# Gated heads: the output experts by routing instead of by a product over all eight experts

## The reference, cut to what matters

```python
# L1 gated heads: 8 heads of 64, 8 experts for each head
q = (x @ w_q).reshape(b, n, 8, 64); k = (x @ w_k).reshape(b, n, 8, 64)
gates = sigmoid((x @ w_gate).reshape(b, n, 8, 8))
gm = one_hot(argmax(gates)) * gates                 # one expert per token and head
values = einsum('bhne,ehdk,bnd->bhnk', gm, value_experts, x)
attn = softmax(causal(q * 64**-0.5 @ k.T))
out = einsum('bhij,bhjk->bhik', attn, values)
out = einsum('bhne,ehkd,bhnk->bhnd', gm, output_experts, out)
x = x + out.sum(heads)
# L0 expert layer, the part touched: gate_logits = tokens @ gate_w.T  (8 experts, top 2)
```

## Time and profile before

| | |
|---|---|
| profiled execution, its own time | 3965.39 us |
| its span | 3963.7 us |
| gated heads begin (POOL's first instruction in them) | 2772.85 us |
| busy over the span | PE 91%, weight loads 76%, DVE 74%, ACT 55%, POOL 8% |
| granted PE clock over the span | 0.964 |
| DMA | 109.74 MB, mean 28 GB/s |
| SP's copies of 128 rows in L0's expert stage, issue to landing | median 2.1 us (L806), 1.9 us (L810) |

### The profile page before, as it was taken

How to read it: one execution, slowest core, us unless ns; L and a number is a source line. 1 busy time by engine, 2 the same in 40 slices (tenths; PEclk the granted TensorE clock), 3 DMA queues, 4 the chain that set the end, 5 groups by cost and what they waited for, 6 DMA issues and landing times. The chain is left out here.

```text
span 3963.7 us, 93437 instructions
## 1 busy us (share of the span) xinstructions
PE 3604.9 (91%) x28994; PEld 2998.0 (76%) x28994; DVE 2943.2 (74%) x9189; ACT 2170.0 (55%) x6661; POOL 299.0 (8%) x382
## 2 busy tenths in 40 slices
PE   6999999899999998269967889998899999999998
PEld 5888888688888887259845666665688888888887
DVE  5666666677777776546558878887888888888886
ACT  5767777677777774135444557776433333333333
POOL 0000000000000000431188000000000000000000
PEclk9999999899999998579989999999999999999999
DMA  2000000100000003332211000000200000000000
GB/s 98 0 0 0 0 0 0 38 33 11 11 11 11 11 11 102 110 109 78 67 55 42 0 20 21 21 21 15 95 9 16 8 11 13 8 11 13 11 11 9
DMA packets 56112, 109.74 MB, mean 28 GB/s; under 512 B 8368, under 2 KB 27184, under 8 KB 55728
## 3 DMA queue, kind: packets, MB, share of 16 engines
q1 hardware_dynamic: 46656, 80.72, 6.5%
q0 software_dynamic: 8464, 26.22, 2.0%
q10 hardware_dynamic: 864, 1.19, 0.1%
HBM read 72.46 MB, written 35.65 MB: 27 GB/s over the span
## 5 line engine op out<-in xcount | busy, mean ns | idle before, releaser
L639 ACT ACTIVATE c_pr<-c_sm,c_nmx 128x256 f32<-128x256 f32 x512 | 254.5, 499 | 153.6 <-DVE c_nmx L485 153.6
L127 PE MATMUL f_ps_out<-f_out_rounded,f_zgT 128*128 128x256 f32 x1024 | 309.7, 302 | 0.0
L128 PE MATMUL f_ps_out<-f_out_rest,f_zgT 128*128 128x256 f32 x1024 | 288.1, 281 | 0.0
L129 PE MATMUL f_ps_out<-f_out_rounded,f_zgT 128*128 128x256 f32 x1024 | 285.9, 279 | 0.0
L639 ACT ACTIVATE a_pr<-a_sm,a_nmx 128x128 f32<-128x128 f32 (+1 forms) x512 | 227.3, 445 | 106.3 <-DVE a_nmx L485 106.2
L485 DVE CUSTOM_DVE_ANT_0 a_sm<-a_ps_s,causal 128x128 f32<-128x128 f32 (+1 forms) x512 | 152.6, 355 | 164.2 <-PE a_ps_s L371 164.2
L2156 DVE TENSOR_REDUCE f_v<-f_gv 128x64 f32<-128x512 f32 x256 | 269.0, 1051 | 0.4
L1747 ACT ACTIVATE c_pr<-c_ps_s,c_nmx 128x256 f32<-128x256 f32 x512 | 214.2, 500 | 88.2 <-DVE c_nmx L1579 88.2
L485 DVE CUSTOM_DVE_ANT_0 c_sm<-c_ps_s,c_mask 128x256 f32<-128x256 f32 x512 | 186.8, 421 | 92.0 <-PE c_ps_s L371 90.4
L2306 ACT CAST f_zgT<-f_ps_g 128x512 fp32r<-128x512 f32 x256 | 151.3, 591 | 182.4 <-PE f_ps_g L2036 182.4
L2147 DVE TENSOR_TENSOR f_gv<-f_ps_v,f_gm_step 128x512 f32<-128x512 f32 x256 | 175.5, 685 | 97.5 <-PE f_ps_v L129 86.0
(11 more groups left out here) (377 smaller groups left out, 11405.2 us busy)
## 6 DMA issues: line engine op xcount, KB each, us to landing
f_slot_rows<-f_run POOLq DMA_DIRECT2D x1, 9216.0 KB, 34.5
f_rows<-f_slot_rows SPq DMA_DIRECT2D x72, 128.0 KB, 2.1
f_slot_out<-f_y SPq DMA_DIRECT2D x72, 128.0 KB, 1.9
c_ctx_stage<-in_ctxT SPq DMA_DIRECT2D x32, 256.0 KB, 2.7
small<-in_f_w SPq DMA_DIRECT2D x16, 512.0 KB
x_sb<-in_x SPq DMA_DIRECT2D x8, 512.0 KB, 8.0
small<-in_c_w SPq DMA_DIRECT2D x8, 512.0 KB, 3.7
c_mask_stage<-in_mask SPq DMA_DIRECT2D x16, 256.0 KB, 2.9
```

The source lines that it names most:

```text
L127: nc.tensor.matmul(out, sh, mh, start=start, stop=False, **kw)
L128: nc.tensor.matmul(out, sh, ml, start=False, stop=False, **kw)
L129: return nc.tensor.matmul(out, sl, mh, start=False, stop=stop, **kw)
L639: last = nc.scalar.activation(pr[:, r, i, 0:n], sm[:, j, i, 0:n], ACT.Exp, bias=nmx[:, j, i:i + 1], scale=-1.0, accum_out=sums[:, r, i:i + 1])
```

## The change

The gated heads are written anew around the output experts; the L0 gate is turned over.

- Order of the steps: batches go in four groups of four, and a **phase** is one pair of heads for the four batches of a group. There are 16 phases of 4 steps. The tokens of a group stay in SBUF (`xs`), so x is read and turned for a whole group ahead of its phases; from the second group on it is read twice, once for the gates and once for the values.
- Values: the same products, but the columns are laid out with the expert innermost, so that `sum_v` reads neighbouring elements, and the gate's value is taken out of them: `gate_v` multiplies by the one-hot choice, and the value of the gate goes into the copy of the probabilities (`take_prT`) and into `scale`. The probabilities are no longer divided on DVE: the inverse of the sum is in `scale`, with which `take_z` multiplies.
- Output: each row (token and head) is sent by an indexed transfer to a slot in DRAM, sorted by expert, with its 64 values twice (512 bytes). A phase has 15 **blocks** of 128 slots for each of its two heads, and a block has one expert. For a block SP loads the rows, PE turns them (two transposes), ACT and DVE split them, PE multiplies with the weights of the block's expert (four products of 256 columns, the expert's number read from a register), ACT copies the result out, and SP stores it. Indexed transfers that add into SBUF bring the rows back to `x_sum`.
- For this the gates' choices are counted: products with a triangle and with ones (`count`), running sums, slots and owners (`index`), all small.
- q and k are made by `product3` of rounded parts in place of four products of full precision.
- The loop over steps is written out: 77 slots, of which the last 13 have no step of their own.
- L0 gate: the gate weights are the stationary side and 256 tokens the moving side, six products a batch; ACT copies the 8 x 256 result and PE turns it back by two transposes, two batches later.

The diff, cut to its core:

```diff
@@ routed_experts, PE: the L0 gate
-                for i in range(ST):
-                    n = ST * b + i
-                    for dc in range(DC):
-                        last = product3(nc, ps_l[:, n * E:(n + 1) * E], [a[:, b % 2, dc, i * P:(i + 1) * P] for a in tT],
-                                        [a[:, dc, :] for a in gate_w], dc == 0, dc == DC - 1)
-                last.then_inc(gated, 1)
+                if b >= 2:
+                    pe.wait_ge(lT_ready, b - 1)
+                for dc in range(DC):
+                    last = product3(nc, ps_h[b % 2][0:E, 0:S], [a[:, dc, :] for a in gate_w],
+                                    [a[:, b % 2, dc, :] for a in tT], dc == 0, dc == DC - 1)
+                last.then_inc(gated, 1)
+            def turn_gates(b):
+                pe.wait_ge(lT_ready, b + 1)
+                for i in range(ST):
+                    n = ST * b + i
+                    last = nc.tensor.transpose(ps_l[:, n * E:(n + 1) * E], lT[:, b % 2, i * P:(i + 1) * P], c.ident[0:E, 0:E])
@@ gated_heads, POOL
+            def scatter(n):
+                pool.wait_ge(indexed, 2 * (n // GB) + 2)
+                pool.wait_ge(z_ready, n + 1)
+                for i in range(ST):
+                    for j in range(2):
+                        t = ST * part(n) + i
+                        pool.indirect_dma_start(rows_z, bass.IndirectOffsetOnAxis(ap=slot_at[:, n // GB % (2 * ROUND), t, j:j + 1], axis=0),
+                                                zr[:, i, j].rearrange("p u k -> p (u k)"), None).then_inc(scattered, 16)
+            def gather(q, k):
+                ...
+                for t in range(half * TG // 2, half * TG // 2 + TG // 2):
+                    done = HEADS * g + 2 * p + j
+                    if done:
+                        pool.wait_ge(summed[t], 16 * done)
+                    pool.indirect_dma_start(x_sum[:, t, :], None, rows_y[q % ROUND],
+                                            bass.IndirectOffsetOnAxis(ap=result_at[:, q % (2 * ROUND), t, j:j + 1], axis=0),
+                                            compute_op=ALU.add).then_inc(summed[t], 16)
+            for n in range(LAST):
+                if 0 <= n - 4 < N:
+                    scatter(n - 4)
+                if 0 <= n - GATHER_AT < N:
+                    gather((n - GATHER_AT) // GB, (n - GATHER_AT) % GB)
@@ gated_heads, PE
-                for p in range(E // 2):
-                    last = product3(nc, ps_out[:, i * D:(i + 1) * D], [t[:, k % 2, p, :] for t in zgT],
-                                    [t[:, 2 * s + j, p, :] for t in w_out], s == 0 and k == 0 and p == 0, ...)
+            def turn_rows(n, step, late_half):
+                pe.wait_ge(rows_in[n % RR], 16 * (n // RR + 1))
+                if n:
+                    pe.wait_ge(sT_ready, n)
+                ...
+                for j in range(2):
+                    last = nc.tensor.transpose(ps_s[0][:, j * P:(j + 1) * P], rows[:, n % RR, j, :], c.ident[:])
+            def experts(n, owner_of):
+                pe.wait_ge(sT_ready, n + 1)
+                if n >= 2:
+                    pe.wait_ge(y_ready, n - 1)
+                for j in range(2):
+                    e = owner_of(j * BLOCKS + m)
+                    for h in range(2):
+                        last = nc.tensor.matmul(ps_y[n % 2][:, j * D:(j + 1) * D], sT[:, h, j, :],
+                                                w_out[:, bass.ds(e + (2 * p + j) * E, 1), :].rearrange("p a d -> p (a d)"),
+                                                start=(h == 0), stop=(h == 1))
+            turn_x(job_at[-GB], -1)
+            for b in range(GB):
+                gates(b)
+                if b + 1 < GB:
+                    turn_x(job_at[b + 1 - GB], -1)
+            for n in range(LAST):    # q, m = (n - 9) // 4, four blocks a slot; at m == 0: pe.load of the owners
+                if now: project(n)
+                blocks(0)
+                if now: project_v(n, 0)
+                ... values(n - 3), turn(n - 2, 0); blocks(1); project_v(n, 1); turn(n - 2, 1); scores(n - 1)
+                ... project_v(n, 2); blocks(2); project_v(n, 3); blocks(3); back(n - 3); gates; count
@@ gated_heads, DVE
-        gv = sb("gv", [P, 2, E, 64])
+        gv = sb("gv", [P, 64, E])
+            def take_z(n):
+                dve.wait_ge(backed, n + 1)
+                dve.wait_ge(scaled, n + 1)
+                if n:
+                    dve.wait_ge(scattered, 64 * n)
+                ...
```

More of the change, by code:

```diff
@@ L1239, in small_heads @@
         if not softmax:
-            gathered = [sem(f"gathered{i}") for i in range(ST)]
+            gathered = [c.kept.enter_context(nc.semaphore(f"{tag}_gathered{i}")) for i in range(ST)]
             weighted = sem("weighted")
@@ new lines, in gated_heads @@
+        chosen_pos = sb("chosen_pos", [P, 2, TG, HEADS])
+        full = sb("full", [P, HEADS, E])
+        ends = [sb(f"ends{n}", [P, HEADS, 4 + E]) for n in range(3)]
+        end = sb("end", [P, 2, HEADS, E])
+        first_row = sb("first_row", [P, 2, HEADS, E])
+        half_of = sb("half_of", [P, HEADS // 2, 2])
+        at = work[:, ST * HEADS * E:].rearrange("p (t j e) -> p t j e", t=TG, j=2)
+        at_sum = sb("at_sum", [P, TG, 2])
+        slot_at = sb("slot_at", [P, 2 * ROUND, TG, 2], U32)
@@ new lines, in _, with blocks @@
+            normalise(0)
+            dve.wait_ge(made, 14)
+            for b in range(GB):
+                rest_x(b)
+                if b + 1 < GB:
+                    normalise(b + 1)
+                choose(b)
+                if b == 0:
+                    rest_qk(0)
+                if b < AHEAD:
+                    pieces.rest(nc, dve, b, b + 1)
+            dve.wait_ge(made_round, 2)
+            for n in range(LAST):
+                def blocks(k):
+                    if (it := place(n, k)) is not None and it[1] < BLOCKS:
+                        rest_rows(it[0] * BLOCKS + it[1])
+                now = n < N
+                if n - 1 in count_at:
+                    take_count(count_at[n - 1])
+                if n in index_at:
+                    index(index_at[n])
+                if 0 <= n - 4 < N:
+                    take_z(n - 4)
+                if 0 <= n - 2 < N:
+                    scale_of(n - 2)
+                blocks(0)
+                if now:
+                    gate_v(n, 0)
+                    sum_v(n, 0)
+                if n in qk_at:
+                    rest_qk(qk_at[n])
+                blocks(1)
+                if now:
+                    gate_v(n, 1)
+                if 0 <= n - 1 < N:
+                    row_max(n - 1, 0)
+                if now:
+                    sum_v(n, 1)
+                if 0 <= n - 1 < N:
+                    row_max(n - 1, 1)
+                if now:
+                    gate_v(n, 2)
+                if n in job_at and job_at[n][2]:
+                    rest_x(job_at[n][3])
+                if now:
+                    sum_v(n, 2)
+                blocks(2)
+                if now:
+                    gate_v(n, 3)
+                blocks(3)
+                if now:
+                    sum_v(n, 3)
+                if n in choose_at:
+                    choose(choose_at[n])
+                if n + 1 in job_at:
+                    normalise(job_at[n + 1][0])
+                pieces.rest(nc, dve, 2 * n + AHEAD, 2 * n + AHEAD + 2)
@@ L2543 @@
     y = nc.dram_tensor("f0_slot_out", (72, P, D), F32, kind="Internal").ap()
-    program(nc, dram, mid, slots, y, out)
+    y1 = [nc.dram_tensor(f"f1_slot_out{n}", (15, P, 2 * D), F32, kind="Internal").ap() for n in range(4)]
+    program(nc, dram, mid, slots, y, y1, out)
     r = run_bass_kernel_spmd(nc, [arrays], core_ids=[0])
```

929 lines of the change are left out of this document (570 added, 359 removed).

## The result

The changed kernel took 4086.07 us in the median of four runs (4078.14 to 4092.36), the kernel before 3972.92 beside it: a ratio of 1.0281 (1.0255 to 1.0308), slower by 2.8%. The forecast was 3740, with 8% for slower. The profiled execution has a span of 4089.3 us. In two later sets of runs, in which the kernel before took 3954 and 3953 us in place of 3973, the same changed kernel was 1.0067 (1.0051 to 1.0084) and 1.0070 (1.0054 to 1.0087) of it. So 2.1 points of the 2.8 depend on where it ran. The forecast of 5.9% less was wrong in both places: where the ratio was 1.007, the span was 3991 us against 3737.

A forecast was written before the change was run, and what follows sets the result against it. PE was taken as the bound, with DVE close under it. 2797.5 + 9 x 11 + 55 x 13.5 + 10 + 106 - 18 = 3737 us span, stated as 3740; own range 3700 to 3785, 8 in 10 within 3665 to 3850.

The forecast's parts named there:

- I add 0.4 a slot: 13.5: Gated heads from the tenth slot: PE and DVE waiting on each other adds 0.4 us to PE's 13.1.
- Work of PE and DVE a slot: Gated heads: PE 13.1 us a slot with blocks, 9.9 without; DVE 10.8, or 11.6 with dependent sums.
- Blocks: Gated heads from the tenth slot: 15 blocks in four slots, 2.6 us of PE a slot plus 0.4 coupling.
- the load of registers: Start of each phase: loading the owners' registers, mostly covered by the projection, 0.6 us times 16, 10 in all.
- POOL's price: Indexed transfers, eight a slot: 1.27 us each, adding ones priced like plain ones, 10.2 a slot, hidden under 13.5.
- rival 2: POOL becomes the bound: an adding gather costs 0.97 more, 2.24 us; a slot 14.0, total 3800; 14%.
- Rivals 2 and 4: The second of these: POOL's adding gathers alone make it slower, 3965 us at 2.9 each, 4145 at 3.6; 8%.
- Rival 3: Gated heads: PE and DVE wait on each other, no engine full, 15.2 us a slot from the tenth, 3830; 21%.
- First nine slots: Start of the gated heads, no blocks or second gates: PE 9.9 us, taken as 11 a slot for DVE's weight splitting.
- First projection: Start of the gated heads: four batches turned ahead instead of one, 15.6 us later, at 2797.5 before L0's saving.
- L0's gate: L0 expert stage: 18 us saved, from 14 at PE's 1.2 GHz to 24 if the clock is at 2.4.
- The end: After the last step: 106 us; last phase's 15 blocks at 2.35 each, done at 80, then four gathers, 20.

The follow-up runs named there:

- after_again: The changed kernel run once more, unaltered, beside a kernel before at 3954 us: 3982.22 us, 1.0067 of it.
- spread2: Changed kernel with rows requested earlier, DVE's output ahead of count and index, small DVE operations spread out, x stores/loads and choice reordered: 3826.69 us, 0.9687 of before.
- early_rows: Changed kernel with SyncE asking for a phase's first three blocks of rows during the phase ahead's last steps: 3904.53 us, 0.9870 of the kernel before.

## Why the prediction was wrong, step by step

**The step that failed** is "I add 0.4 a slot: 13.5", an average coupling for every slot. Just ahead of it stands that slots with `index`, `choose` or `take_count` "put 3 to 5 us more on DVE", and that only two quarters' value products can be buffered; it was not drawn from this that PE waits for nearly all of it. The slot with gates and index has 6.3 us of DVE operations ahead of `take_z`, and PE stood 4.6. In `after_again` the slots with gates cost 117 us over 13.5 and the phases' first ones 56; in `spread2` the same slots are 37 and 1 over. The mended orders took 142 of the 952.5 us of the 55 slots away with the same work.

- Work of PE and DVE a slot: near. Without blocks plain slots are 10.5, the shortest 9.9, against 9.9; with them 13.7 against 12.9 (the 13.5 less the 0.6 of gates and turning). DVE was busy 10.6 us a slot from the tenth on (580 us in `after_again`) against 10.8, and `sum_v` was at 0.68 in the first profile, where the earlier trace rows had led to 0.69:

```profile
L2471 DVE TENSOR_REDUCE f_v<-f_gv 128x64 f32<-128x512 f32 x193 | 131.7, 682 | 17.4 <-PE f_ps_z L2262 12.3 <-issue 2.6 <-DVE f_gv L2462 0.2
```

- Blocks: 3.2 us a slot against 3.0, in plain slots. At the start of a phase the prediction looked for the cost in the load of registers (10 us in all); it was SyncE's order: 4 to 5 us of wait a phase, and 5.9 us of these slots (19.1 to 13.2 in `early_rows`). That a request stands behind a store in a queue could be read from the code; the prediction followed no queue of SyncE.
- POOL's price: the adding transfer is 1.56 + 0.30, not 1.27, between the forecast and rival 2's 2.24. The Trainium skill (Collectives: The Full Stack, the part on why ReduceScatter is half of AllGather) speaks of two source reads for an add. The prediction had read that as twice the length on POOL; it grew to 1.6 times (1.56 against 0.96). Rivals 2 and 4 did not happen: a slot of POOL is 4 x 1.27 + 4 x 1.86 = 12.5 of 13.7, close, but never what ended a wait of the steps.
- Rival 3 had the right sign, both engines under 88%, and the wrong picture and size: an even 15.2 (3830), where it was 13.7 with slots of 19 to 24 between.
- First nine slots: 125 against 99. Slots 4, 6 and 8 (counted from 0), with gates, are 21.2, 21.0 and 19.5 us beside neighbours of 10.5 and 11.0. PE waits 21.6 us for `f_zr` in the nine, behind the same row of DVE operations, uncounted there; in `spread2` it is 7.9, and the nine take 115.5. The rest of the 26 was not taken apart.
- First projection: the forecast went by a kernel before of the first place, so it is to be held against 2782.2 there: 3 us late, by two errors that nearly cancel, which is luck. L0's gate gave 24 us and not 18, and so the turning of four batches in place of one took about 24 us more and not 15.6 (2782.2 - 2781.9 + 24). For L0 the granted clock rose to full in the third batch (24 was the bound for that case). The first row is the stretch at the gates (clock 0.82, where the earlier trace rows had 0.50), the others are starts of the turning of x: 3.5 us for two batches where the earlier trace rows had 3.33 for one.

```profile
1552.00:1572.00 20.00, 17.87 (x116) 11.98 (x116) 15.30 (x43) 11.70 (x31) 0.29 (x1) 0.82 1.01 342
```

```profile
1562.25 0.66 PE L879 MATMUL f_ps_x<-ident,f_t 128*128 128x128 f32 x4
1563.76 0.66 PE L879 MATMUL f_ps_x<-ident,f_t 128*128 128x128 f32 x4
1565.76 0.66 PE L879 MATMUL f_ps_x<-ident,f_t 128*128 128x128 f32 x4
```

- The end: 149 against 106. The 15 last blocks run alone at 2.9 us each where 2.35 were counted (the terms named for it add up to 2.4). PE is at 1.2 GHz there (clock 0.50): from the start of a block's turning to ACT it is 0.7, and the products take 1.0 to the next turning, where 0.6 was counted for PE. The copy of the result (0.59), which was counted in, runs beside this chain. Both of the last phases do so and not one; they are done 114 us after the last slot, not 80. The last 16 transfers back take 30 us, not 20. Rows of `after_again`, from one block's turning to the next one's:

```profile
3920.79 0.63 PE L2282 MATMUL f_ps_s<-ident,f_rows 128*128 128x128 f32 x2
...
3921.51 0.38 ACT L2643 CAST f_sT<-f_ps_s 128x256 fp32r<-128x256 f32 x1
...
3921.93 0.42 DVE L2511 TENSOR_TENSOR f_sT<-f_ps_s,f_sT 128x256 fp32r<-128x256 f32 x1 [2.49 <-ACT f_sT L2643]
...
3922.69 1.22 PE L2299 MATMUL f_ps_y<-f_out_rounded_rest,f_sT 128*128 x4 [1.27 <-DVE f_sT L2511]
3923.71 0.63 PE L2282 MATMUL f_ps_s<-ident,f_rows 128*128 128x128 f32 x2
```

```profile
3900.00:3930.00 30.00, 14.52 (x54) 10.71 (x53) 3.40 (x8) 7.31 (x17) 22.55 (x16) 0.50 0.79 176
```

Against the span of `after_again` the terms add up: 3737 - 15 + 26 + 200 + 43 = 3991, where the -15 is 3 late, as said, and 18 less for the place. The first profile has 98 more: 18 ahead of the gated heads, where before has its holes too, 77 in the 55 slots and 3 behind. The holes could have been asked about from the kernel before: 41 us of unknown waits beside its 64 fetches, and the change adds 512 indexed transfers. The size could not be had from it: between the two places the kernel before differs by 19 us, the gated heads of the changed one by 80.

## What to carry to other kernels

In a pipeline written out by hand an average hides what costs most: list the slots by kind, and for each kind look at the longest run of small operations ahead of one that another engine waits for, and at what can be buffered meanwhile. Follow each transfer queue in its own order: a request behind a store, or behind a wait for a landing, costs the whole latency although its data is ready. And an unknown releaser in the profile before calls for a term and a chance of its own, if the change multiplies what stands beside it.

## What was not expected of the hardware

- An indexed transfer that adds into SBUF holds POOL 1.56 us, a plain one 0.96, for the same 128 rows of 1 KB; with it left plain, the slots that begin a phase with an exposed row load are 1.8 us shorter (19.1 to 17.3).
- In one of two places where the program ran, DVE and ACT stood still, mostly for 2 to 3 us at a time, beside POOL's indexed transfers; the slots from the tenth on grew there by 0.18 us for each transfer, by count. In the other place they never did. That the transfers make the holes was not shown. The kernel before differs by 19 us between the two, the changed one by 104.
- In the kernel before, the granted clock was 0.50 (1.2 GHz) over 20 us of L0's gates in which PE was busy without a gap. With the gates written as products of 256 columns it was full (2.4 GHz) from 1560 us on, after the third batch. Why it stayed low before is open.
